# A two-network GNN block: 48 early tiles in front of the branch, the head in another order, and 16-bit keys

## The reference

```python
N, D, R = 3125, 128, 8                     # 53125 edges (17 per node on average), sorted by dst
h = jnp.maximum(_layernorm(x), 0.0)
for W, root, b in layers:                  # three relational layers
    out = h @ root + b
    for r in range(R):
        msg = jnp.where((edge_type == r)[:, None], (h @ W[r])[src], 0)
        cnt = segment_sum(edge_type == r, dst, N)
        out = out + segment_sum(msg, dst, N) / jnp.maximum(cnt, 1.0)[:, None]
    h = relu(out)
x = x + h
h = jnp.maximum(_layernorm(x), 0.0)
h = relu((h + segment_sum(h[src], dst, N)) @ W1 + b1) @ W2 + b2
out = batchnorm(h) * gamma + beta + x
```

## Time and profile before

| | us |
|---|---|
| median of three runs | 1685.67 (1683.42 to 1686.53) |
| the profiled execution | 1682.43 |
| its span in the profile | 1680.6 |

### The profile page before, as it was taken

One profiled execution on the slowest core, in us unless ns is written; L12 is line 12 of the kernel. 1 busy time (PEld: TensorE's weight loads), 2 busy tenths in 40 slices (PEclk: granted clock), 3 DMA queues, 4 the chain that ended last, 5 costly groups with the idle time before them and its releaser, 6 DMA issues.

```text
span 1680.6 us, 17006 instructions
## 1 busy us (share of the span) xinstructions
PE 1170.9 (70%) x4448; PEld 775.0 (46%) x4448; DVE 868.2 (52%) x3241; ACT 645.3 (38%) x1137; POOL 1186.0 (71%) x1256
## 2 busy tenths in 40 slices
PE   3799565657566777777777878765667666666777
PEld 1357444435344544444454545544545454544543
DVE  4647855455555177787778777751222222222213
ACT  4520500000000278888888888860011111212224
POOL 0757777777777577777777777757777777777770
PEclk9899755555555555758575756575567776768898
DMA  6963544353533311323232323231111111111111
GB/s 169 314 231 106 184 130 134 123 162 100 164 116 93 100 54 54 96 60 97 59 98 59 98 59 97 67 98 52 53 52 53 52 54 52 53 52 53 53 53 40
DMA packets 81154, 159.35 MB, mean 95 GB/s; under 512 B 24337, under 2 KB 38556, under 8 KB 77724
## 3 DMA queue, kind: packets, MB, share of 16 engines
q0 software_dynamic: 39936, 81.87, 18.4%
q1 hardware_dynamic: 39354, 74.73, 12.5%
q10 hardware_dynamic: 1762, 1.59, 0.4%
HBM read 115.33 MB, written 42.77 MB: 94 GB/s over the span
## 4 chain that ended last, share of the span: by engine, by line
POOL 67%; issue 22%; PE 5%; DMA 3%; ACT 1%; ACTq 1%; DVE 1%; SPq 0%; POOLq 0%; DVEq 0%
POOL rows L1034 67%; PE ps_h L438 3%; DMA h_table<-stage 2%; DMA rows<-h_table,idx 1%; PE ps_agg L464 1%; DMA early<-in_dst_t 1%; ACTq L1067 1%; ACT early L598 0%; PE ps_agg L1483 0%; ACT stage L614 0%; PE ps_h L558 0%; PE ps_agg L541 0%; PE ps_a L558 0%; PE ps_a L564 0%; PE ps_h L529 0%
## 5 line engine op out<-in xcount | busy, mean ns | idle before, releaser
L1034 POOL DMA_INDIRECT rows<-h_table,idx x1208 | 1143.5, 947 | 398.5 <-issue 367.2
L464 PE MATMUL ps_agg<-sel,rows 128*128 128x64 f32 (+12 forms) x2786 | 718.8, 375 | 443.5 <-DMA rows<-h_table,idx 433.1
L464 PEld LDWEIGHTS ps_agg<-sel,rows 128*128 128x128 f32 x2786 | 605.3, 278 | 737.8 <-DMA rows<-h_table,idx 586.3
L796 DVE TENSOR_SCALAR sel<-iota,early,norm 128x64 f32<-128x64 f32 x1208 | 358.0, 329 | 435.4 <-PE ps_agg L464 433.6
L891 DVE TENSOR_TENSOR early<-ps_a,early 128x300 f32 x416 | 197.8, 475 | 126.2 <-PE ps_a L509 115.4
L702 ACT ACTIVATE scratch<-scratch,ones 128x300 bf16<-128x300 f32 x416 | 223.2, 536 | 50.4 <-PE ps_a L509 42.6
L708 ACT ACTIVATE scratch<-iota,code_lo 128x300 f32<-128x300 f32 x416 | 226.4, 545 | 12.5
L438 PE MATMUL ps_h<-w_all,xT 128*128 128x512 f32 x300 | 197.8, 772 | 16.7 <-ACT stage L614 16.7
L775 DVE TENSOR_SCALAR_CACHE_REDUCE agg_s<-scratch,key_f 128x256 bf16<-128x256 f32 x416 | 194.2, 472 | 27.1 <-DMA scratch<-key_rows 16.7
L509 PE MATMUL ps_a<-scratch 128*128 128x300 bf16 x416 | 169.7, 409 | 0.9 <-DVE early L891 0.9
L880 DVE TENSOR_SCALAR scratch<-iota,code_lo 128x128 bf16<-128x128 f32 x416 | 145.1, 349 | 0.0
(11 more groups left out here) (128 smaller groups left out, 546.0 us busy)
## 6 DMA issues: line engine op xcount, KB each, us to landing
h_table<-stage SPq DMA_DIRECT2D x150, 256.0 KB, 2.5
scratch<-key_rows SPq DMA_DIRECT2D x26, 1088.0 KB, 6.1
rows<-h_table,idx POOLq DMA_INDIRECT x1208, 2.5
x_rows<-in_x SPq DMA_DIRECT2D x6, 256.0 KB, 7.1
x_table<-early SPq DMA_DIRECT2D x6, 256.0 KB, 3.0
out<-early SPq DMA_DIRECT2D x6, 256.0 KB
w_all<-in_W SPq DMA_DIRECT2D x2, 512.0 KB, 4.2
early<-x_table,early POOLq DMA_INDIRECT x40, 4.0
```

Source lines behind the costliest of these rows:

```text
L464: mm = nc.tensor.matmul(sums_of(L, k)[:, at:at + width], rows[:, G % SLOTS, :], sel[:, G % SELS, in_window:in_window + width], start=False ...
L796: done = nc.vector.tensor_scalar(mine, here, dst, norm[:, t:t + 1], ALU.is_equal, ALU.mult)
L1034: pool.indirect_dma_start(rows[:, slot, :], None, table, bass.IndirectOffsetOnAxis(ap=column, axis=0)).then_inc(landed, 16)
```

## The change

- The first 48 tiles are early ones, 8 more (`FORE`). Their windows start at `fore_start`, even steps of 60 nodes per batch, and need 7 banks instead of 6. In `head_order` two early tiles follow a table tile (`FORE_PACE`), so the head has 18 table tiles instead of 28.
- POOL gathers x for the early tiles in front of the branch: it waits for the x0 stores and no longer for the flag.
- The queue of ACT starts with dst, type and src alone. W[0] moves to SP behind x. The four shifted loads of dst are issued after all norms and the first copy into `xT`, with a semaphore of their own, and DVE treats the shifted columns after its last norm. Norm 1 no longer stands behind them.
- SP: five x0 stores stand before the key rows, two behind. The twelve small loads (roots, biases, GIN weights and vectors) go between the stores of table 0's first seven blocks, which are now in front of the branch; chunks 2 and 3 behind blocks 13 and 20; W of layers 1 and 2 behind the whole table, with a semaphore that PE waits for at layer 1's first block.
- PE puts the product for the flag behind group 1. ACT's cast of `iota` goes behind group 2, the copy of the keys behind group 5's first step. DVE matches 32 tiles before it needs `iota` (8 before).
- `key_rows`, `key_turn`, `halo` and the two chunk buffers are 16-bit integers instead of 32-bit floats, so a chunk's broadcast is half the bytes. `key_f`, with which they are compared, stays 32 bits.

```diff
--- before.py
+++ after.py
...
@@ -53,8 +54,9 @@
-FORE = 40
+FORE = 48
 FORE_RING = 12
+FORE_PACE = 2
@@ -85,11 +87,15 @@
     GROUPS = cdiv(BLOCKS, 4)
+    assert REL * (PAD_NODE + 1) < 2 ** 15
...
     start_of = [P * (t - t % BATCH) // DEG - LEAD + STEP * (t % BATCH) for t in range(TILES)]
-    SLACK = max(P * t // DEG - LEAD - start_of[t] for t in range(TILES))
+    FORE_STEP = start_of[BATCH] - start_of[0]
+    fore_start = [FORE_STEP * (t // BATCH) + STEP * (t % BATCH) - LEAD for t in range(FORE)]
+    assert all(fore_start[t] <= start_of[t] for t in range(FORE))
+    SLACK = max(P * t // DEG - LEAD - s for t, s in [*enumerate(start_of), *enumerate(fore_start)])
@@ -140,33 +146,31 @@
     assert FORE % BATCH == 0
-    FORE_STEP = start_of[BATCH] - start_of[0]
-    assert all(start_of[t] == FORE_STEP * (t // BATCH) + STEP * (t % BATCH) - LEAD for t in range(FORE))
...
-        s, found = start_of[t], []
+        s, found = fore_start[t], []
...
-    KEY_BANKS = cdiv(start_of[FORE - 1] + SPAN, KEY_BANK)
+    KEY_BANKS = cdiv(fore_start[FORE - 1] + SPAN, KEY_BANK)
...
     head_order = [("fore", t) for t in range(FORE_RING)]
-    for t in range(FORE_RING, FORE):
-        head_order += [("tile", FORE + t - FORE_RING), ("fore", t)]
-    HEAD = 2 * FORE - FORE_RING
+    for t in range(FORE_RING, FORE, FORE_PACE):
+        head_order += [("tile", FORE + (t - FORE_RING) // FORE_PACE)] + [("fore", f) for f in range(t, t + FORE_PACE)]
+    HEAD = FORE + (FORE - FORE_RING) // FORE_PACE
...
-    key_rows = nc.dram_tensor("key_rows", (1, HALO + COLS * P), F32, kind="Internal").ap()
+    key_rows = nc.dram_tensor("key_rows", (1, HALO + COLS * P), I16, kind="Internal").ap()
...
@@ -231,23 +235,22 @@
-        key_turn = shared(4 * P).rearrange("p (q k) -> p q k", k=P)
...
-        fore_at = shared(FORE).bitcast(I32)
-        key_near = shared(FORE)
+        fore_at = rest[:, 0:FORE].bitcast(I32)
+        key_near = rest[:, FORE:2 * FORE]
...
@@ -431,6 +437,8 @@
                 elif b == span_of[L - 1][sums_with[L - 1][b]][0]:
+                    if b == 0 and L == 1:
+                        pe.wait_ge(s_wr, 16 * (GIN - 1))
@@ -931,7 +939,8 @@
-        CHUNK_BEHIND = {10: 2, 19: 3}
+        SP_BRANCH = 7
+        CHUNK_BEHIND = {13: 2, 20: 3}
@@ -955,16 +964,9 @@
                 load_x(g)
-            for L in range(GIN):
-                if L:
-                    sp.dma_start(w_all[:, L, 0:REL, :], w_rel[L].rearrange("r f o -> f r o")).then_inc(s_w, 16)
-                sp.dma_start(w_all[:, L, REL, :], root_w[L]).then_inc(s_w, 16)
-                sp.dma_start(vecs[:, L:L + 1], bias_w[L].rearrange("(p o) -> p o", o=1)).then_inc(s_w, 16)
-                store_x0(L)
-            sp.dma_start(w_gin[:, 0, :], gin_w1).then_inc(s_w, 16)
-            sp.dma_start(w_gin[:, 1, :], gin_w2).then_inc(s_w, 16)
-            for n, v in enumerate((gin_b1, gin_b2, gamma, beta)):
-                sp.dma_start(vecs[:, 3 + n:4 + n], v.rearrange("(p o) -> p o", o=1)).then_inc(s_w, 16)
+            sp.dma_start(w_all[:, 0, 0:REL, :], w_rel[0].rearrange("r f o -> f r o")).then_inc(s_w0, 16)
+            for g in range(5):
+                store_x0(g)
@@ -972,20 +974,36 @@
             sp.dma_start(key_rows[0:1, 0:HALO], halo[:]).then_inc(s_key_out, 16)
-            for g in range(GIN, GROUPS):
+            for g in range(5, GROUPS):
...
             load_chunk(sp, 1)
+            small_loads = [(w_all[:, L, REL, :], root_w[L]) for L in range(GIN)]
+            small_loads += [(vecs[:, L:L + 1], bias_w[L].rearrange("(p o) -> p o", o=1)) for L in range(GIN)]
+            small_loads += [(w_gin[:, 0, :], gin_w1), (w_gin[:, 1, :], gin_w2)]
+            small_loads += [(vecs[:, 3 + n:4 + n], v.rearrange("(p o) -> p o", o=1))
+                            for n, v in enumerate((gin_b1, gin_b2, gamma, beta))]
+            for b in range(SP_BRANCH):
+                store_rows(sp, 0, b)
+                for into, what in small_loads[2 * b:2 * b + 2]:
+                    sp.dma_start(into, what).then_inc(s_w, 16)
+            assert 2 * SP_BRANCH >= len(small_loads)
...
             fast = sp.value_load(flag[0:1, 0:1], min_val=0, max_val=1)
+
+            def load_w():
+                for L in range(1, GIN):
+                    sp.dma_start(w_all[:, L, 0:REL, :], w_rel[L].rearrange("r f o -> f r o")).then_inc(s_wr, 16)
+
             with sp.If(fast != 0):
-                for b in range(BLOCKS):
+                for b in range(SP_BRANCH, BLOCKS):
...
                         load_chunk(sp, c)
+                load_w()
@@ -1025,6 +1044,12 @@
             nc.gpsimd.iota(iota_i, pattern=[[1, EARLY + NP]], base=-EARLY, channel_multiplier=0).then_inc(s_pool_const, 1)
+            pool.wait_ge(s_src, 32)
+            pool.wait_ge(s_x0, 16 * GROUPS)
+            for t in range(FORE):
+                pool.indirect_dma_start(fore_rows[:, t, :], None, x0_table,
+                                        bass.IndirectOffsetOnAxis(ap=src_i[:, t:t + 1], axis=0)
+                                        ).then_inc(s_fore_row[t // BATCH], 16)
...
@@ -1062,38 +1081,35 @@
             act.dma_start(src_i[:], src_t[:, 0:COLS]).then_inc(s_src, 16)
-            act.dma_start(w_all[:, 0, 0:REL, :], w_rel[0].rearrange("r f o -> f r o")).then_inc(s_w0, 16)
-            act.dma_start(dst_i3[0:P - 1, 1, :], dst_t[1:P, 0:COLS]).then_inc(s_edges, 16)
-            act.dma_start(dst_i3[0:HALO, 2, :], dst_t[HALO:P, 0:COLS]).then_inc(s_edges, 16)
-            act.dma_start(dst_i3[HALO:P, 2, :], dst_t[0:HALO, 1:COLS + 1]).then_inc(s_edges, 16)
-            act.dma_start(dst_i3[P - 1:P, 1, :], dst_t[0:1, 1:COLS + 1]).then_inc(s_edges, 16)
...
             scalar_norm(act, 0)
-            scalar_sd(act, 2)
-            scalar_norm(act, 1)
-            scalar_xT(act, 0)
             whole = COLS // P
-            for g in range(3, GROUPS):
+            for g in range(2, GROUPS):
...
                 scalar_norm(act, g - 1)
-                if g == 4:
+                if g == 5:
...
             scalar_norm(act, GROUPS - 1)
+            scalar_xT(act, 0)
+            act.dma_start(dst_i3[0:P - 1, 1, :], dst_t[1:P, 0:COLS]).then_inc(s_shifted, 16)
+            act.dma_start(dst_i3[0:HALO, 2, :], dst_t[HALO:P, 0:COLS]).then_inc(s_shifted, 16)
+            act.dma_start(dst_i3[HALO:P, 2, :], dst_t[0:HALO, 1:COLS + 1]).then_inc(s_shifted, 16)
+            act.dma_start(dst_i3[P - 1:P, 1, :], dst_t[0:1, 1:COLS + 1]).then_inc(s_shifted, 16)
...
                     evacuate(act, nc.scalar.copy, 0, b, 1)
-                if g == 0:
+                if g == 2:
...
                     nc.scalar.copy(iota[:], iota_i).then_inc(s_iota, 1)
-            act.wait_ge(s_w, 16 * (2 * GIN + 2 + 6))
+            act.wait_ge(s_w, 16 * (GIN + GIN + 2 + 4))
@@ -1169,13 +1185,13 @@
             norm_x(dve, 0)
-            dve.wait_ge(s_edges, 80)
-            nc.vector.tensor_scalar(dst_pad, dst_i3[:], 0.0, float(PAD_NODE + 1), ALU.is_lt, ALU.mult
+            dve.wait_ge(s_edges, 16)
+            nc.vector.tensor_scalar(dst_pad[:, 0, :], dst_i3[:, 0, :], 0.0, float(PAD_NODE + 1), ALU.is_lt, ALU.mult
...
             dve.wait_ge(s_edge_f, 1)
-            nc.vector.tensor_tensor(dst_f3[:], dst_i3[:], dst_pad, ALU.add).then_inc(s_edge_f, 1)
+            nc.vector.tensor_tensor(dst_f, dst_i3[:, 0, :], dst_pad[:, 0, :], ALU.add).then_inc(s_edge_f, 1)
@@ -1185,6 +1201,13 @@
             dst, after, far = (dst_f3[:, n, 0:TILES] for n in range(3))
+            dve.wait_ge(s_shifted, 64)
+            nc.vector.tensor_scalar(dst_pad[:, 1:3, :], dst_i3[:, 1:3, :], 0.0, float(PAD_NODE + 1), ALU.is_lt, ALU.mult
+                                    ).then_inc(s_edge_f, 1)
+            dve.wait_ge(s_edge_f, 4)
+            nc.vector.tensor_tensor(dst_f3[:, 1:3, :], dst_i3[:, 1:3, :], dst_pad[:, 1:3, :], ALU.add
+                                    ).then_inc(s_edge_f, 1)
+            dve.wait_ge(s_edge_f, 5)
@@ -1209,7 +1232,6 @@
             nc.vector.tensor_scalar(flag[:, 0:1], ps_total[:, 0:1], 0.0, None, ALU.is_equal).then_inc(s_flag, 1)
-            dve.wait_ge(s_iota, 1)
@@ -1224,7 +1246,8 @@
-                match_to(BATCH)
+                match_to(min(CHUNK * 2, FORE + BATCH))
+                dve.wait_ge(s_iota, 1)
@@ -1233,7 +1256,7 @@
                         match_to(s + BATCH + 1)
-                    for f in range(FORE_RING + t - FORE, min(FORE_RING + t - FORE + BATCH, FORE)):
+                    for f in range(FORE_RING + FORE_PACE * (t - FORE), min(FORE_RING + FORE_PACE * (t - FORE + BATCH), FORE)):
...
@@ -1385,12 +1409,12 @@
                 table0(g)
-                if g == 0:
+                if g == 1:
...
                                      ).then_inc(s_total, 1)
-            pe.wait_ge(s_w, 16 * (2 * GIN + 2 + 6))
+            pe.wait_ge(s_w, 16 * (GIN + GIN + 2 + 4))
```

More of the change, by code:

```diff
@@ L10 @@
 I32 = mybir.dt.int32
+I16 = mybir.dt.int16
 U8 = mybir.dt.uint8
@@ L198, in gnn_kernel @@
         ones = sb("ones", [P, P])
```

(17 more changed lines are left out.)

## The result

The changed kernel takes **1666.74 us** (median of 4 runs, 1665.2 to 1668.91) beside 1686.1 for the kernel before (4 runs, 1683.42 to 1687.78): ratio 0.9888, 95% interval 0.987 to 0.9905. It is faster by 19.4 us, where I had forecast 10.5. The profiled execution took 1665.2, its span is 1663.4, 17.2 less than the span of the earlier trace rows.

The account below looks back on a forecast made before the run. Bound taken: POOL's layer-0 gathers, 1.25 us each, and their start. Start 9.5 us earlier, eight gathers fewer 10.0, new waits 9.0 back: 10.5 us, 1682.4 to 1671.9; median forecast 1675, own range 1669 to 1680, stated range 1662 to 1687.

Parts of the forecast that it names:

- the early-landing rival: Shifted load has its DMA engine nearly alone, lands by 31 to 33; POOL starts at 86.7; 19 us gained, 1666.5; chance 0.21.
- landing: Arrival of the 127-row shifted load of dst, slowed on one DMA engine by stores: forecast 42, bounds 31 and 56.
- the 17 blocks: Blocks of table 0 on PE behind its wait for the flag's sum: 41.0 us forecast, where 42.7 before.
- the waits: POOL's new layer-0 waits for PE before the 41st and 49th table gathers: 4.1 and 5.5 us, taken as 9.0.
- early gathers: POOL's 48 gathers of x, starting once x0 stores land: 24.5 to 85, hidden behind table 0.
- sum of the test ready: End of DVE's shifted-column work and checks, which PE awaits after 8 blocks of table 0: 8.4 us after landing, 50.4.
- the holes: Idle gaps in the 17 blocks behind two key chunks: 11.7 us before, 5.7 taken off for 16-bit keys, bounds 0 and 9.
- Late landing: Rival: shifted load lands at 56 or later, POOL starts at 109.3; 3.5 us slower, 1689; chance 0.13.
- No effect on the start: Rival: the earlier start gains only what new POOL waits take back; eight gathers alone count, 1675.7, inside the forecast.
- the ring: Limit of 32 slots that POOL's gathers may be ahead of PE in layer 0; its new waits were taken as 9.0 us.
- The port: Rival: DVE's 16-bit matches hold what POOL needs to write descriptors, 0.1 us more per gather, +37 us, 1712; chance 0.03.
- Edits at nothing: Moved W loads, twelve small loads, W0 on SP and chunk 4, each priced at nothing.

Follow-up runs that it names:

- The cut: The changed kernel with its 127-row shifted load cut into 112 and 15 rows: 1660.0 us, 4.9 below the changed kernel run beside it.
- The pairs: The changed kernel with PE telling POOL of freed slots every 2 tiles instead of every 8: 1660.34 us, 4.5 below the changed kernel run beside it.

## Why the prediction was right, point by point

The direction and the mechanism held: an earlier start and eight gathers fewer give, a new wait takes. The time lies in the stated range of 1662 to 1687, but only because that range takes in the early-landing rival too; the forecast's own range, 1669 to 1680, was missed. The size was off by 8 us in the better direction. In the traces the start came 4.1 us earlier than forecast (landing 3.5 and the 17 blocks 3.1 earlier, less 2.7 between PE and POOL) and the waits took 3.6 us less (5.4 instead of 9.0).

| step | forecast | measured |
|---|---|---|
| norm 1 | 9.8 | 9.65 |
| first copy ends | 21.3 | 20.5 |
| ACT held in an issue | 3 | 4.65 |
| early gathers | 24.5 to 85 | 29.25 to 90.6 |
| shifted load in | 42 | 38.5 |
| sum of the test ready | 50.4 | 46.9 |
| 17 blocks of table 0 | 41.0 | 37.9 |
| PE ends table 0 | 91.9 | 85.2 |
| first table gather | 95.3 | 91.2 |
| PE's head | 71.8 | 69.0 |
| waits of POOL for PE | 4.1 + 5.5 | 0 + 5.4 |
| eight gathers fewer | 10.0 | 10.0 |

- **The landing, 3.5 us early.** The picture fits (one engine of sixteen, slowed by its turns with stores), but the count of rows in slow turns was too high; ACT stood 4.65 us in its issue, so the stores came late. DMA in 18 to 40, 40 slices of 0.55 us, shows the load nearly alone (ninth to eleventh value), then the stores beside it:

```profile
GB/s 96 289 233 52 55 296 162 82 27 24 23 49 182 215 372 277 184 87 97 136 248 331 385 397 394 390 402 382 386 386 418 315 173 169 31 226 369 227 179 348
```

  23 to 27 GB/s at 22.4 to 24, as the 20 to 25 in the earlier trace rows. The cut confirms the cause: 112 + 15 rows are in 12.7 us sooner. So the rule of the Trainium skill that I cited (DMA: Bandwidth & Descriptors, section "Why a DMA increments its semaphore by 16 and not by 1") is borne out here: 127 rows from the ACT queue go as over one engine of sixteen, and the same rows cut in two do not.

  What I had not seen is that the landing was hardly the last thing that PE waited for. I had the first eight blocks done near 41 (27 + 14), well before the sum; they ended at 44.9, because ACT waited 6.17 us and 2.18 us for stores between 29 and 40, and PE then stood only 1.67 us for the sum. An earlier landing by itself was worth no more than that. The cut moved the product by 8.6 us because these waits shrank with it (to 2.95 us at most).
- **The stretch of 17 blocks, 3.1 us short.** From 47.23 to 85.16. The clock was 0.95 on average in 48 to 85, so the 1.5 us that I gave to the clock were nearly unused; the rest is in the holes, whose longest fell from 6.29 to 3.08. How much of that the 16 bits did and how much the order, no run settles.
- **Early gathers, 4.7 us late: the step that failed.** I let the x0 stores land 3 us after their issue. The last one took 8.3 us (DMA issues of the changed kernel in 18 to 40):

```profile
x_table<-early SPq DMA_DIRECT2D x1, 64.0 KB, 8.3
```

  In all eight runs of the changed kernel's head with the row load whole it took 8.2 to 8.5 us, in the three with the load cut 2.7 to 3.0. So the row load holds it; that its part on the busy engine stood in turn with the row load is my reading. "The early gathers, done at 85, hide in this" is wrong by as much: they end at 90.6, and POOL then waits only 0.66 us for the table. In this run the error cost nothing, since the table was not there before 91.2; but two limits stood within a us of each other, and I had priced one.
- **From PE's end of table 0 to POOL's start, 6.1 us for 3.4.** SP's queue after, then the last store before:

```profile
86.47 0.32 SPq L920 DMA_DIRECT2D h_table<-stage  x1
86.96 0.32 SPq L922 DMA_DIRECT2D h_table<-stage  x1
87.32 1.68 SPq L997 DMA_DIRECT2D w_all<-in_W  x2
```
```profile
102.25 0.32 SPq L914 DMA_DIRECT2D h_table<-stage  x1
```

  The last store is issued 1.8 us after PE's end (0.9 before), and POOL starts 4.3 us after that (2.6 before): the two W loads, 512 KB each, run beside it (DMA share 0.98 in 86 to 92). The later issue is no matter of W: before its last two copies ACT stood 1.75 us for a store of an earlier block, where before the change this was 0.39. I had put W at nothing with PE's layer 1 in view, and not looked at the stores in front of it. No run moved W away, so its share of the 1.7 us is argued.
- **The waits, 3.6 us too long.** POOL started 2.7 us later behind PE than I had it, and the head was 2.8 us shorter. Both work on the first wait, which vanished (PE was through the 16th table tile at 140.3, 55.1 us after its start, and the 41st gather followed at once at 142.3); the second, forecast at 5.5, was 5.4. The pairs confirm that the wait was in the sum: 4.5 us come back.
- **Rivals.** The measured time is what the early landing was to give (1666.5), but that is chance, for its mechanism did not occur: the load landed at 38.5, not 31, and the table gathers started at 91.2, not 86.7. Of the missing 4.5 us 3.6 came from the shorter wait, and the medians differ by 2.2 us more than the profiled executions do. Late landing: no. No effect on the start (1675.7): no, the start gained 13.6 us and the ring took 5.4 back. The port: 354 matches on 16-bit input in 92 to 555, and the gathers take 0.948 us each there against 0.946 in the earlier trace rows, so no contention that counts; a match is 0.471 us against 0.473 in the earlier trace rows.
- **Edits at nothing.** The twelve small loads and chunk 4: no wait of POOL names them. DVE waits 9.6 us once for a chunk, until 84.3, beside the table, and PE has no wait for DVE behind it. DVE's waits for PE went from 106.7 us to 98.1.

## What to carry to other kernels

Price every queue that can end last at a join, not only the one that ends last today: here POOL's early gathers and the table arrived within a us of each other, and the cheap next step (cutting one load, 4.9 us; a finer signal, 4.5; together 11.6) lay in what the change had made late. Cut a load of 127 rows into 112 + 15 (12.7 us sooner here). A ring that signals in batches of 8 takes back part of what an earlier start gives (2.3 of 8.5 us with the cut).

## What the runs showed of the hardware

- A load of 127 rows (207 KB) from ACT's queue costs others too: the next issue on that queue stood 4.6 to 4.9 us (8.92 in the earlier trace rows), and 0.75 to 0.88 once the load was cut; and a 64 KB store issued from SP at about 20 landed 8.2 to 8.5 us later, against 2.7 to 3.0 with the load cut.
- Another Trainium2 chip ran the same kernels 21% slower, in eight runs. In its head, idle time put down to issue stood on PE, ACT and DVE while a long row of indirect gathers ran (14.4 of 37 us busy on PE, against 32.4 on the first chip); most of the 21% came later and stays unexplained.
